# Attention of a four-layer sequence kernel: probabilities turned once as plain fp32, sums for four heads in four column quarters, V unsplit

## What is computed

```python
B, T, D, H = 4, 1024, 512, 16            # 16 heads of 32
xn = layer_norm(x, norm_w, norm_b)
q = (xn @ q_w + q_b).reshape(B, T, H, 32)
k = (xn @ k_w + k_b).reshape(B, T, H, 32)
att = einsum('bnhl,bmhl->bnmh', q, k)     # no scale
att = softmax(att + (1 - mask) * -1e6, axis=m)
v = ((xn @ v_w + v_b) * mask).reshape(B, T, H, 32)
y = einsum('bnmh,bmhl->bnhl', att, v)
x = x + silu(modulated layer_norm(y)) @ out_w + out_b
```

## Time and profile before

| | us |
|---|---|
| median of 3 runs | 7054.1 (7051.11 to 7069.93) |
| the profiled execution, span of the trace | 7066.8 |
| p0, first transposes to last V operation | about 100 to 480 |
| attention, first load to last store issued | 483.5 to 1902.5 |
| TensorE busy in the span | 5969.9 (84%) |
| VectorE busy | 5019.0 (71%) |
| ScalarE busy | 4532.6 (64%) |
| DMA, mean over the span | 132 GB/s |

### The profile page before, as it was taken

One profiled execution on the slowest core, in us unless ns is written; L12 is line 12 of the kernel. 1 busy time (PEld: TensorE's weight loads), 2 busy tenths in 40 slices (PEclk: granted clock), 3 DMA queues, 4 the chain that ended last, 5 costly groups with the idle time before them and its releaser, 6 DMA issues. The chain is left out here.

```text
span 7066.8 us, 89203 instructions
## 1 busy us (share of the span) xinstructions
PE 5969.9 (84%) x31488; PEld 4032.8 (57%) x31488; DVE 5019.0 (71%) x6369; ACT 4532.6 (64%) x6817; POOL 2481.1 (35%) x1098
## 2 busy tenths in 40 slices
PE   6989999999889847899857888886999668888883
PEld 2448888888644344344346666663444356666661
DVE  2449999999742164445589999994455399999992
ACT  1228888888621042455478989893555399999991
POOL 0000000000000000000079999994000099999993
PEclk8999999999989978999989999998999899999996
DMA  5442222222242244333455666563243465655554
GB/s 195 170 152 61 73 66 75 64 73 61 77 155 97 103 151 149 120 140 136 160 153 157 173 161 164 153 161 108 96 153 140 156 156 154 156 155 152 154 144 171
DMA packets 608856, 935.18 MB, mean 132 GB/s; under 512 B 104985, under 2 KB 252569, under 8 KB 607909
## 3 DMA queue, kind: packets, MB, share of 16 engines
q1 hardware_dynamic: 596964, 904.27, 42.4%
q0 software_dynamic: 5120, 16.78, 0.7%
q10 hardware_dynamic: 6336, 8.52, 0.3%
HBM read 590.40 MB, written 338.98 MB: 132 GB/s over the span
## 5 line engine op out<-in xcount | busy, mean ns | idle before, releaser
L1618 POOL TENSOR_TENSOR scan_hC<-scan_h,scan_Crep 128x1024 f32<-128x1024 f32 x1024 | 2394.5, 2367 | 2805.5 <-DVE scan_h L1785 2777.3
L1729 ACT ACTIVATE scan_a<-scan_dt,scan_A 128x512 f32<-128x512 f32 x2048 | 1368.3, 698 | 90.7 <-DVE scan_h L1785 73.7
L1652 PE MATMUL scan_y<-ident,scan_hC 128*128 128x128 f32 x8192 | 1116.7, 280 | 294.4 <-POOL scan_hC L1618 288.9
L1652 PEld LDWEIGHTS scan_y<-ident,scan_hC 128*128 128x128 f32 x8192 | 906.0, 142 | 683.0 <-POOL scan_hC L1618 635.5
L1785 DVE TENSOR_TENSOR_SCAN scan_h<-scan_a,scan_carry,scan_h 128x512 f32<-128x512 f32 x1024 | 1217.0, 1258 | 23.9 <-ACT scan_a L1729 21.2
L1785 DVE TENSOR_TENSOR_SCAN scan_h<-scan_a,scan_h 128x512 f32<-128x512 f32 x1024 | 1154.7, 1197 | 58.2 <-ACT scan_a L1729 57.8
L1705 ACT COPY scan_h<-scan_drive 128x1024 f32<-128x1024 f32 x1024 | 1042.4, 1018 | 173.1 <-PE scan_drive L1640 159.3
L1640 PE MATMUL scan_drive<-scan_Bd,scan_dT 128*128 128x256 f32 x4096 | 751.7, 306 | 132.5 <-ACT scan_h L1705 80.1
L805 DVE TENSOR_TENSOR att_pTlo<-att_TP,att_pThi 128x512 fp32r<-128x512 f32 x1024 | 657.6, 683 | 128.2 <-ACT att_pThi L843 126.5
L1640 PEld LDWEIGHTS scan_drive<-scan_Bd,scan_dT 128*128 128x128 f32 x4096 | 559.4, 193 | 185.1 <-issue 99.4
L843 ACT CAST att_pThi<-att_TP 128x512 fp32r<-128x512 f32 x1024 | 547.8, 587 | 178.8 <-PE att_TP L738 172.5
(11 more groups left out here) (151 smaller groups left out, 6812.1 us busy)
## 6 DMA issues: line engine op xcount, KB each, us to landing
scan_dT<-scratch_dtuT SPq DMA_DIRECT2D x512, 256.0 KB, 5.5
scratch_dtuT<-ssmin_dT SPq DMA_DIRECT2D x128, 512.0 KB, 2.9
scan_Crep<-scratch_bc SPq DMA_DIRECT2D x64, 1024.0 KB, 9.5
att_q<-scratch_q_split SPq DMA_DIRECT2D x256, 128.0 KB, 3.0
att_k<-scratch_k_split SPq DMA_DIRECT2D x256, 128.0 KB, 3.2
scratch_uD<-ssmin_uD SPq DMA_DIRECT2D x64, 512.0 KB, 3.4
scratch_z<-ssmin_zt SPq DMA_DIRECT2D x128, 256.0 KB, 2.1
scratch_dt<-ssmin_dt SPq DMA_DIRECT2D x64, 512.0 KB, 2.6
```

Of the source, the lines that this page charges most:

```text
L1618: nc.gpsimd.tensor_tensor(hC[k % 2][:], of, Crep[:, 2 * p:2 * p + 2, :], ALU.mult).then_inc(s["scaled"].handle, 1)
L1652: last = nc.tensor.matmul(y[j][:, t, :], hC[k % 2][:, i, t * P:(t + 1) * P], ident[:], start=(p == 0 and i == 0 and t == 0), stop=False, i ...
L1729: nc.scalar.activation(a[(2 * k + i) % 3][:], dt[j][:], ACT.Exp, scale=A[:, m, 2 * p + i:2 * p + i + 1]).then_inc(s["decayed"].handle, 1)
```

## The change

- V is stored once, as plain fp32 of 512 columns per token, in `scratch_v`. Rounding and rest (L572, L573) and the tiles `whole` are gone from `project`; Q and K stay split.
- Units are reordered: in a group of four heads the head j is now innermost, u = ((group c) * 8 + t) * 4 + j. Q and K have 8 slots, one for each head of two groups, and a slot is loaded again when its head's last score of the group is done.
- The turned probabilities are copied once, unrounded: the left half of TP by ScalarE (`take_left`), the right half by VectorE (`take_right`), into pT, a ring of 8 tiles of 128x1024, one per unit. `turn(u)` waits for left_taken and right_taken of unit u-1.
- `weigh(g, part)` sums four units (the four heads at one query tile) in four parts of two key tiles, one part per unit of the loop: 8 plain fp32 matmuls with V's 32 columns of head j as weights and 128 columns of pT moving, into rows 32j to 32j+31 of YT.
- YT is then 128 (head and channel) x 128 (query). It is copied by ScalarE (two tiles `yts` now) and turned back with one 128x128 transpose. `fold` is gone.
- SP loads Q and K of all four heads of a group before the next V; the order at the start is head 0, mask, heads 1 to 3, V.

```diff
-        k, q = ring("k", 3, [P, T]), ring("q", 3, [P, T])
-        v = ring("v", 2, [P, TT, 4, 2 * DH])
+        HG = 4
+        GROUPS = B * H // HG
+        k, q = ring("k", 2 * HG, [P, T]), ring("q", 2 * HG, [P, T])
+        v = ring("v", 2, [P, TT, HG, DH])
...
-        pT = [ring(f"pT{part}", 2, [P, 2, T]) for part in ("hi", "lo")]
+        pT = ring("pT", 2 * HG, [P, T])
...
             def turn(u):
                 w(pe, "exped", u + 1)
                 for half in range(2):
                     if u >= 1:
-                        w(pe, "lo_taken", 2 * u - 1 + half)
+                        w(pe, ("left_taken", "right_taken")[half], u)
...
+            def weigh(g, part):
+                c = g // TT
+                if part == 0:
+                    w(pe, "left_taken", HG * g + HG)
+                    if g % TT == 0:
+                        pe.wait_ge(v_in[c % 2].handle, v_in[c % 2].at(16 * (c // 2 + 1)))
+                    if g >= 1:
+                        w(pe, "yt_copied", g)
+                if part == 2:
+                    w(pe, "right_taken", HG * g + HG)
+                for m in range(2 * part, 2 * part + 2):
+                    for j in range(HG):
+                        last = nc.tensor.matmul(YT[DH * j:DH * j + DH, 0:P], v[c % 2][:, m, j, :],
+                                                pT[g % 2 * HG + j][:, m * P:(m + 1) * P], start=(m == 0), stop=(m == TT - 1))
...
-                for n in range(4):
-                    last = nc.tensor.matmul(Y[:, n, :], yts[:, n, :], fold[:], start=True, stop=True)
-                last.then_inc(s["y_turned"].handle, 1)
...
+                nc.tensor.transpose(Y[:, 0:P], yts[g % 2][:], ident[:]).then_inc(s["y_turned"].handle, 1)
...
-            for u in range(U):
+            for u in range(U + 7):
                 if u + 3 < U:
                     scores(u + 3)
-                turn(u)
-                if u >= 2:
-                    weigh(u - 2)
-                if u >= 7 and u % 4 == 3:
-                    turn_back((u - 7) // 4)
...
+                if u < U:
+                    turn(u)
+                if u >= HG + 1 and (u - HG - 1) // HG < G:
+                    weigh((u - HG - 1) // HG, (u - HG - 1) % HG)
+                if u >= 10 and u % HG == 2:
+                    turn_back((u - 10) // HG)
...
+            def take_right(u):
+                w(dve, "turned", 2 * u + 2)
+                if u >= 2 * HG:
+                    w(dve, "weighed", u // HG - 1)
+                nc.vector.tensor_copy(pT[u % (2 * HG)][:, HALF:], TP[:, HALF:]).then_inc(s["right_taken"].handle, 1)
...
+            def take_left(u):
+                w(act, "turned", 2 * u + 1)
+                if u >= 2 * HG:
+                    w(act, "weighed", u // HG - 1)
+                nc.scalar.copy(pT[u % (2 * HG)][:, 0:HALF], TP[:, 0:HALF]).then_inc(s["left_taken"].handle, 1)
```

More of the change, by code:

```diff
@@ L432, in project, with part_of, value_of @@
         parts = [sb(f"parts{k}", [P, 2 * HALF]) for k in range(8)] if split else None
-        whole = [sb(f"whole{k}", [P, HALF]) for k in range(2)] if split else None
         hi_done = core.count("hi_done")
[L436 to L439, removed]
+        def part_of(slot, s):
+            return parts[slot][:, s * HALF:(s + 1) * HALF]
+        def value_of(slot):
+            return part_of(slot, 0) if split else stage[slot][:]
         banks = [psum(f"bank{k}", [P, HALF]) for k in range(8)]
@@ L567, in _ @@
                         dve.wait_ge(core.slot_in[slot].handle, core.slot_in[slot].at(u * 16 + 16))
[L568 to L573, removed]
+                        ins = nc.vector.tensor_tensor(value, value, res[slot][:], ALU.add)
                     ins.then_inc(staged[slot].handle, 1)
@@ L607, in _ @@
                     else:
-                        tile = parts[slot][:] if split else stage[slot][:]
-                        width = tile.shape[1]
-                        dst = job["dst"][it, b * P:(b + 1) * P, a * width:(a + 1) * width]
+                        tile, dst = value_of(slot), job["dst"][it, b * P:(b + 1) * P, a * D:(a + 1) * D]
                     sp.dma_start(dst, tile).then_inc(stored[slot].handle, 16)
@@ L650, in attention @@
         TP = psum("TP", [P, T])
[L651 to L654, removed]
+        YT = psum("YT", [P, HALF])
+        Y = psum("Y", [P, HALF])
+        kq_in = core.slot_in[0:8]
+        v_in, mask_in = ([core.count(f"att_{n}_in{j}") for j in range(2)] for n in ("v", "mask"))
+        s = {n: core.count(n) for n in ("mneg_ready", "exped", "turned", "left_taken", "right_taken", "y_ready",
                                         "yt_copied", "y_turned")}
@@ L825, in _ @@
                 if u >= 1:
-                    take_lo(u - 1)
+                    take_right(u - 1)
                 if u + 2 < U:
                     shift(u + 2)
-                if u >= 9 and u % 4 == 1:
-                    take((u - 9) // 4)
-            take_lo(U - 1)
+                if u >= 11 and u % HG == 3:
+                    take((u - 11) // HG)
+            take_right(U - 1)
             take(G - 2)
@@ L860, in _ @@
                 if u >= 1:
-                    copy_hi(u - 1)
-                if u >= 6 and u % 4 == 2:
-                    copy_yt((u - 6) // 4)
-            copy_hi(U - 1)
+                    take_left(u - 1)
+                if u >= 9 and u % HG == 1:
+                    copy_yt((u - 9) // HG)
+            take_left(U - 1)
+            copy_yt(G - 2)
             copy_yt(G - 1)
-    for n in ("scored", "shifted", "exped", "weighed"):
-        s[n].stage_added(U)
+    for n, per in (("scored", U), ("shifted", U), ("exped", U), ("turned", 2 * U), ("left_taken", U), ("right_taken", U),
+                   ("weighed", G), ("yt_copied", G), ("y_turned", G), ("y_ready", G), ("mneg_ready", B)):
+        s[n].stage_added(per)
     for j in range(2):
@@ L871, in attention @@
         mask_in[j].stage_added(16 * (B // 2))
-        v_in[j].stage_added(16 * B * H // 8)
-    for j in range(3):
-        kq_in[j].stage_added(128 * len(range(j, B * H, 3)))
+        v_in[j].stage_added(16 * GROUPS // 2)
+    for j in range(8):
+        kq_in[j].stage_added(128 * GROUPS // 2)
     core.vector_step.stage_added(G)
```

163 lines of the change are left out of this document (66 added, 97 removed).

## The result

The changed kernel takes 6807.78 us (median of 4 runs, 6799.88 to 6812.9) against 7054.47 for the kernel before in the same series (4 runs): a ratio of 0.9642, 95% interval 0.963 to 0.9654. I had forecast 6999 with a range of 6890 to 7230. The sign was right, the size was not: 247 us less instead of 55, and outside the range on the fast side.

The account below looks back on a forecast made before the run. All three engines were taken to be within 0.16 us of attention's 2.73 us unit, with TensorE next to bound. A 2.61 us unit gave -61, the start +8, the projection -2: -55, so 6999 us, range 6890 to 7230.

Parts of the forecast that it names:

- The sign: Whole kernel: faster by over 0.3% (21 us) at chance 0.52, within that 0.11, slower 0.37.
- The bound now: Attention before the change: all three engines within 0.16 us of the 2.73 us unit, VectorE and ScalarE 2.7, TensorE 2.57.
- The sums: TensorE, eight sum matmuls per attention unit: quarters side by side, 0.92 us, bounded by 0.86 and 1.85.
- Rival D: Attention sums: later quarters overlap both records of a matmul, sums 0.43, unit about 2.2 us, whole 6790 us; chance 0.05.
- The changes of shape: TensorE, twice per attention unit: 0.09 us into the quarters and 0.20 out to the full array.
- Turning back: TensorE, attention: one 128x128 turn per four units, 0.11 us, or 0.03 per unit.
- The new wait: Attention: first copies of a group wait for sums still reading pT; about 0.1 us each four units, 0.03 per unit.
- VectorE and ScalarE: Attention after the change: 2.1 and 2.05 us of work per unit, near 75% busy, neither bounding.
- Around the cycle: Outside the attention cycle: loads of heads 2 and 3 cost 8 us at the start; the projection's end saves 2.
- Together: Sum of TensorE's terms per attention unit: 2.61 us against 2.73, 61 us less over 512 units.

Follow-up runs that it names:

- e2: Changed kernel with V's 128 columns of all four heads as weights of each sum matmul, in the full array; 7386.36 us.
- e4: Changed kernel with ScalarE and VectorE each copying its half of TP twice, first into a spare tile; 6957.87 us.
- e3: Changed kernel with the head as outer and the key tile as inner loop in each part of the sums; 6829.24 us.
- e11: Changed kernel with the four heads summing in two column quarters instead of four, YT copied in four pieces; 7053.58 us.
- e1: Changed kernel with all four heads summing into rows 0 to 31 of YT, one column quarter; 7480.86 us.
- e8: Changed kernel with 12 pT tiles instead of 8, order otherwise the same; 6756.48 us, ratio 0.956 to the kernel before.
- e5: Changed kernel with the parts of a sum issued two at a time, in every second unit; 6788.45 us, ratio 0.9622 to the kernel before.
- e9: Changed kernel with 12 pT tiles and sum parts issued two at a time, in every second unit; 6723.33 us, ratio 0.9517 to the kernel before.
- e10: Changed kernel with 12 pT tiles and all four sum parts issued in one unit of four; 6789.69 us, ratio 0.9605 to the kernel before.
- e6: Changed kernel with sums ahead of the turn and YT copied ahead of ScalarE's half of TP; 6759.14 us, ratio 0.9569 to the kernel before.

## Why the prediction was right or wrong, point by point

- **The bound now.** Right in kind, wrong in the figures. I had added up record lengths, but a record starts before the one ahead of it on its engine ends, so the sums for VectorE and ScalarE came out too long. Busy time, kernel before:

```profile
900.00:1200.00 300.00, 295.00 (x2197) 254.59 (x2196) 271.78 (x494) 254.20 (x466) 3.63 (x1) 1.00 0.26 63
```

  That is 2.47 us of a unit for VectorE and 2.31 for ScalarE, where I had 2.7 for both: not all three within 0.16 us of the period, but TensorE nearest and VectorE 0.26 below. e2 (plain sums without quarters, +335 us) and e4 (the others kept loaded, 94 us gained of 247) show both sides of it.
- **The sums: the step that failed.** "If a record in another quarter may run beside the second record of the matmul ahead ... one matmul costs about one record: 8 x 0.115 = 0.92." That quarters run side by side was right; the term measured 0.44 (four sets of 0.11) instead of 0.92. It rested on a rule that I had not read from any row, that records start in program order: then a quarter's second record holds up all the other quarters, and only two records ever run together. e3 shows that they don't start in that order across quarters, and e11 that with two quarters in use the time is 0.87. This one term is 0.48 us per unit, 246 us, more than the whole miss of 191. It was bounded below by 0.86, "8 x 256 columns", which takes for granted what was in question; the honest lower bound was 1.85 / 4 = 0.46. Rival D had the 0.43 for the sums, at a chance of 0.05. Its 6790 us is near the 6807.78 in part by luck: it let VectorE's 2.1 with waits set 2.2, but VectorE's work is 1.91 of the 2.23, and the rest above 2.11 is TensorE's wait and the turn back. That the sign came out right is little credit, with 0.52 for faster. The Trainium skill's "TensorE: Matmul & The Clock Gate", section "Part 3", spoke for the fast side: its three quarters at 2.38 times would have given 0.78; here four quarters need four sets where one needs sixteen records, both 0.109 apart, so 4.0 times in a stream, and 1.93 / 0.65 = 3.0 times if the last record's length is counted. I had its number and took a slower one.
- **The changes of shape.** Predicted 0.09 in and 0.20 out. In the changed kernel's trace the eighth turn starts 0.76 behind the first (1001.13), the next record was due at 1001.24, and the first sum record starts at 1001.33 and is 0.02 longer: 0.12. The way out: the last set starts near 1001.69, due 1001.79; scores start at 1001.91 with 0.10 of extra length: 0.21. Together 0.33 against 0.29; e1 against e2 gives 0.28 in dense units. Prices from two other stages of the old trace held here. I had written that the forecast is wrong if a change costs over 0.2; the way out is at 0.21, which is not what made it wrong.
- **Turning back.** 0.06 per four units instead of 0.11, fine.
- **The new wait.** Placed and explained rightly; priced at about 0.1 in four units, measured 0.35. ScalarE's copy starts at 1002.10, 0.31 us after the last set made room for a next (1001.79), takes 0.59, and the turn follows 0.14 later: 1.04. Against it stand 0.69 for the way out and the scores (I had 0.67). The two handoffs were the mis-sized part, 0.45 instead of 0.2. e8 takes the wait out and gains 0.09 per unit, 51 us.
- **VectorE and ScalarE.** 257 and 235 of 300 us busy, 86% and 78%; I had written near 75% of a longer unit. In work per unit that is 1.91 and 1.75 us, where I had 2.1 and 2.05, again from record lengths that overlap. VectorE's copy took 0.69, the upper end of its bounds. Neither bounds the changed kernel, as predicted; e5, e9 and e10 show how close behind their handoffs are.
- **Around the cycle.** ScalarE's wait for the first turn is 8.07 us, against 0.89 in the kernel before: 7.2 more, where I had 8. The four heads' loads were issued 0.46 apart to 495.46 with no long one among them as the earlier trace rows had; the first turn, which stands behind the fourth head's scores on TensorE, starts at 504.9. The projection's last V operation ends at 478.15 instead of 480.42: 2.3, predicted 2.
- **Together.** 2.61 - 0.48 (sums) + 0.04 (shapes) + 0.05 (wait, turn back) = 2.22, and 2.23 with the wait at the start.

## What to carry to other kernels

Small matmuls that write different column quarters ran side by side here in both orders tried, so price them by the busiest quarter's records, and give each neighbour its own quarter. The price is two changes of the array's shape, 0.33 us a pair here: bundle the small matmuls, but only as far as the other engines' buffers last (with a third group of tiles two parts gained 0.07 us a unit and four lost 0.06). To find what a bundle will run into, add up the ring of handoffs, too, and not only each engine's work: turn, copy, turn took 1.36 us here. And add up busy time, not record lengths. When a term has no row, its lower bound must come from the mechanism that one doubts, not from the one assumed.

## What the runs showed of the hardware that I had not expected

- Records of different quarters start independently of program order: 16 in 0.39 us with each quarter's four issued in a row (e3), 16 in 0.38 alternating; in one quarter 0.11 apart (e1). With their order alternating the first four are 7 ns apart, otherwise 13.
- A plain fp32 matmul of 128 columns, 0.22 us in a single quarter (e1), costs 0.055 when all four are in use (0.44 for eight). The fp32r matmul of 256 columns that it replaces, of which a unit had eight too, cost 0.115, and needed the operands split.
- With scores ahead of the sums and a turn behind them (e6) instead of a turn ahead and scores behind, the two changes of shape cost 0.06 us less at most: the dense units are 2.05 and 2.11.
